# Four of ten top-32 masks move from VectorE to ScalarE in a one-core attention kernel

## The chip, the cores and the metric

The kernel runs as one program on one NeuronCore of a Trainium2 chip. The metric is the device time of one execution in microseconds (us). A core has TensorE (PE, matrix products; PEld is its weight loads), VectorE (DVE), ScalarE (ACT), GpSimd (POOL) and a queue for transfers on SyncE (SP). They run side by side and are ordered by semaphores that the program writes out.

## The reference, cut to what matters

A deformable convolution, two transformer layers and a mixture of experts run on 8 images of 64 channels and 56 x 56 positions. The change touches only the attention of the two layers. Each layer has 64 (image, head) pairs, "heads" below, with 3136 queries, 3136 keys and 8 values per key:

```python
scores = jnp.einsum('bhqd,bhkd->bhqk', q, kk) * scale      # 3136 x 3136 for each head
vals, idx = jax.lax.top_k(scores, k)                       # k = 32
w = jax.nn.softmax(vals, axis=-1)
vg = jnp.take_along_axis(v[:, :, None, :, :], idx[..., None], axis=3)
out = jnp.einsum('bhqk,bhqkd->bhqd', w, vg)
```

The kernel never makes indices. It finds each query's 32nd largest score, marks every key below it in a mask, and lets TensorE add a very large negative number to the marked scores before the exponential.

## The kernel before, in words

`heads` calls `attend` 8 times a layer, each for 8 heads. A head has 25 tiles of 128 queries (the last has 64), so one `attend` has 200 tiles and the program 3200. All of the order is written out by hand in one loop for each engine.

**First half: the threshold.** TensorE (`scores`, L242) multiplies a tile's queries with all keys in four pieces (two banks of 448 keys, two, two, one), always into the same two PSUM banks. ScalarE (`keep`, L371) copies each piece to the ring `S` in SBUF, which has 8 slots of one tile. TensorE may not overwrite the banks before that copy is done, and ScalarE's next copy waits for TensorE. VectorE takes the top 8 of each of 28 chunks of 112 keys (`part_top`, L446), merges these candidates to the 32 largest (`candidates`, L463 to L476), tests for doubt (L480) and writes the mask `Z` (L486), which is 1 where the score is below the 32nd. The merge, the test and the mask of a tile are woven into the next tile's chunk maxima.

**Doubt and search.** The candidates are exact unless a chunk hides a ninth large score or the lower tiers of the chunks hold more than eight. `doubt` (L480) marks rows in which that may be so. TensorE counts the marks of a group of four tiles (`flag`, L250; the last group has five), and three tiles later VectorE reads the count (`check`, L496, L497). If there is a mark, VectorE searches the marked tile anew over all 3136 keys (`search`, L515 to L522). When a check is done, VectorE's queue is drained (L506), and `s_free` gives the group's ring slots back to ScalarE.

**Second half: the output.** It works on 512 queries at a time, a set of four tiles, and runs about eight tiles behind the first half. TensorE computes the transposed scores of 256 keys (`fill`: L280, and L289 for the masks, whose blocks are the stationary operand of 128 x 128 matmuls), ScalarE takes the exponential (`exps`, L392 and L395), and TensorE multiplies with the values after every second unit of this kind (`values`, L325). Two such units are in flight in PSUM: `fill(e+2)` waits for `exps(e)`. There are 80 units for the 100 pieces of a head, so four pieces out of five have a unit behind them. Rarer steps are `shifts`/`shift_rows` (L260, L377), `sums` (L403) and `fold`/`folded` (L335, L410).

**The loop that the change cuts into.** In step `a` ScalarE's queue holds `keep(a)` and then `exps(e)`. TensorE's queue holds `scores(a+1)`, `fill(e+2)` and, for every second unit, `values(e)`. Each engine executes its own queue in order.

Of the kernel before, what the change touches and what calls it, by code (L numbers as in the profile page):

```python
# [62 lines left out]
RANKED = TOP_AT + 8 * CHUNKS  # L63
RING = 8
MASKS = 10
BLOCK = 8
PIECES = (2, 2, 2, 1)
AP = len(PIECES)
# [3 lines left out]
PENDING = 4  # L72
CHECKS = [range(4 * g, 4 * g + 4) for g in range(5)] + [range(20, NT)]
LATE = 3
TERMS, ZERO_TO, MAX_AT = 48, 96, 96


# [26 lines left out]
def attend(nc, m, base, n):  # L104

    bank = m.bank
    names = ("q_in", "v9_in", "v1_in", "a_mm", "a_ev", "s_free", "tops", "step", "found", "viol", "flag_mm", "flag_in",
             "z_done", "part", "maxp", "max_mm", "max_in", "e_mm", "e_exp", "pv", "o_ev", "fold_mm", "os_done", "o_out")
    with semaphores(nc, *names) as sems, nc.Block() as block:
        (q_in, v9_in, v1_in, a_mm, a_ev, s_free, tops, step, found, viol, flag_mm, flag_in,  # L110
         z_done, part, maxp, max_mm, max_in, e_mm, e_exp, pv, o_ev, fold_mm, os_done, o_out) = sems
        psO, psX = bank[6], bank[7]
        flags = psX[32:33, :]
        maxima = psX[MAX_AT:MAX_AT + 3, :]
# [24 lines left out]
        def side(i):  # L139
            return i % 2  # L140
# [1 line left out]
        def slot(t):  # L142
            return t % RING

        def place(i, t):
            return (NT * i + t) % MASKS

        def checks_to(i, t):

# [76 lines left out]
        def _(pe):  # L226
# [37 lines left out]
            def fill(e):  # L264

                s, p = units[e]
                i, g = sets[s]
                w = set_width(g)
                per = QW // w
                if p == 0 and i >= 0:  # L270
                    pe.wait_ge(max_in, max_sets(i) + g + 1)
                    pe.wait_ge(s_free, checks_to(i, set_tiles(g)[-1]))
                    pe.wait_ge(z_done, NT * i + set_tiles(g)[-1] + 1)
                if e >= 2:
                    pe.wait_ge(e_exp, e - 1)

                def shifted(x, k):
                    rows = tile_rows(k)
                    at = w * (x % per)
                    pe.matmul(bank[2 + 2 * (e % 2) + x // per][0:rows, at:at + w],  # L280
                              m.K[0:MAX_AT + 3, side(i), 128 * k:128 * k + rows],
                              m.Q[0:MAX_AT + 3, side(i), QW * g:QW * g + w], start=True, stop=False)

                def masked(x, k):
                    rows = tile_rows(k)
                    for j, t in enumerate(set_tiles(g)):
                        cols = tile_rows(t)
                        at = w * (x % per) + 128 * j
                        mm = pe.matmul(bank[2 + 2 * (e % 2) + x // per][0:rows, at:at + cols],  # L289
                                       m.Z[:, place(i, t), 128 * k:128 * k + rows], m.NEG[:, 0:cols],  # L290
                                       start=False, stop=(j == len(set_tiles(g)) - 1))
# [12 lines left out]
                mm.then_inc(e_mm, 1)  # L304
# [57 lines left out]
        def _(act):  # L362
            def keep(a):
                tile, c = divmod(a, AP)
                i, t = divmod(tile, NT)
                rows, at, w = tile_rows(t), CW * sum(PIECES[:c]), PIECES[c]
                act.wait_ge(a_mm, a + 1)
                if c == 0 and tile >= RING:
                    act.wait_ge(s_free, checks_to(*divmod(tile - RING, NT)))
                    act.wait_ge(z_done, tile - RING + 1)  # L370
                act.copy(m.S[0:rows, slot(tile), at:at + CW * w].rearrange("p (a n) -> p a n", a=w),  # L371
                         m.AB[0:rows, 0:w, 0:CW]).then_inc(a_ev, 1)

            def shift_rows(i, g):
                k = max_sets(i) + g
# [36 lines left out]
            for a in range(SLOTS):  # L412
                if a < NA:
                    keep(a)
                for e in units_at(a):
                    exps(e)
                    if e + 3 in first_unit and e + 3 < NE and sets[units[e + 3][0]][0] >= 0:
                        shift_rows(*sets[units[e + 3][0]])
                    if e - 1 in first_unit[1:]:
                        sums(first_unit.index(e - 1) - 1)  # L420
                    if e - 5 in first_unit[1:]:
                        folded(first_unit.index(e - 5) - 1)
            sums(len(sets) - 1)
            for s in range(len(sets)):
                if first_unit[s + 1] + 5 >= NE:
# [6 lines left out]
        def _(dve):  # L432
# [6 lines left out]
                count[0] += 1  # L439
                op().then_inc(step, 1)  # L440

            def part_top(tile, k):
                rows = tile_rows(tile % NT)
                if k % 8 == 0:
                    dve.wait_ge(a_ev, AP * tile + k // 8 + 1)
                ins = dve.max(m.C[0:rows, tile % 2, TOP_AT + k:RANKED:CHUNKS],  # L446
                              m.S[0:rows, slot(tile), CHUNK * k:CHUNK * k + CHUNK])
                if k == CHUNKS - 1:
                    ins.then_inc(tops, 1)

            def candidates(tile):

# [24 lines left out]

                def doubt():
                    dve.wait_ge(found, tile + 1)
                    dve.scalar_tensor_tensor(m.VI[0:rows, t:t + 1], m.C8[0:rows, t:t + 1], C[:, 7:8],  # L480
                                             m.M8[0:rows, side(i), t, 31:32], ALU.max, ALU.is_ge).then_inc(viol, 1)

                def mask():
                    if mask_freed(tile):
                        dve.wait_ge(e_mm, mask_freed(tile))
                    dve.tensor_scalar(m.Z[0:rows, place(i, t), :], m.S[0:rows, slot(tile), :],  # L486
                                      m.M8[0:rows, side(i), t, 31:32], None, ALU.is_lt, saturate=False).then_inc(z_done, 1)
                return steps + [final, doubt, mask]

            def check(i, g):  # L490

# [6 lines left out]
                dve.wait_ge(flag_in, 2 * done)  # L498
                flagged = nc.vector.value_load(m.FI[32:33, 31:32], min_val=0, max_val=128)
                with nc.vector.If(flagged > 0):  # L500
                    dve.wait_ge(z_done, NT * i + checked[-1] + 1)
                    for t in checked:
                        n_t = nc.vector.value_load(m.FI[32:33, t:t + 1], min_val=0, max_val=128)
                        with nc.vector.If(n_t > 0):
                            search(i, t)
                dve.drain().then_inc(s_free, 1)  # L506

            def search(i, t):
                rows = tile_rows(t)
# [4 lines left out]
                for r in range(1, 4):  # L514
# [1 line left out]
                    dve.drain()  # L516
                    dve.max(M8[:, 8 * r:8 * r + 8], S)  # L517
                    dve.drain()
                Z = m.Z[0:rows, place(i, t), :]
                dve.tensor_scalar(Z, S, M8[:, 31:32], None, ALU.is_lt, saturate=False)  # L520
                dve.drain()
                dve.scalar_tensor_tensor(Z, S, LOW, Z, ALU.is_gt, ALU.mult, saturate=False)  # L522
# [2 lines left out]
            for tile in range(TILES):  # L525
                steps = candidates(tile - 1) if tile else []
                for k in range(CHUNKS):
                    part_top(tile, k)
                    for g in range(len(CHECKS)):
                        before = tile - LATE - CHECKS[g][-1]  # L530
                        if k == 6 and before >= 0 and before % NT == 0:
                            check(before // NT, g)
                    if k % 2 == 1 and steps:
                        steps.pop(0)()
                for remaining in steps:
                    remaining()
            if n:
                for remaining in candidates(TILES - 1):
                    remaining()
                check(n - 1, len(CHECKS) - 1)  # L540


Q_TERMS = ((0, 0, 1, 3), (24, 1, 1, 2), (40, 2, 1, 1))
# [11 lines left out]
def attend_memory(nc, ctx, m):  # L555
    for name, shape, dt in (
            ("Q", [128, 2, TOK], BF16), ("K", [128, 2, TOK], BF16), ("V9", [128, NT * (HD + 1)], F32),
            ("V1", [128, 2, NT, 32], F32), ("S", [128, RING, TOK], F32), ("Z", [128, MASKS, TOK], FP8),
            ("W", [128, 4, 2, QW], F32), ("O4", [128, QW], F32), ("OS", [HD + 1, 2, QW], F32),
            ("C", [128, 2, RANKED], F32), ("C8", [128, NT], F32), ("M8", [128, 2, NT, 32], F32),  # L560
            ("VI", [128, NT], F32), ("FI", [33, 32], I32), ("P", [128, 2, 3, 4], BF16), ("R", [128, 2, 4], F32),
# [4 lines left out]
def heads(nc, m):  # L566

    with ExitStack() as ctx:
        attend_memory(nc, ctx, m)
        with semaphores(nc, "zeroed", "spare", "loaded", "v9_first") as (zeroed, spare, loaded, v9_first), nc.Block() as block:  # L570
            @block.gpsimd
            def _(pool):
                for t in (m.V1, m.Q, m.K, m.Z, m.M8, m.VI):
                    pool.memset(t[:], 0.0).then_inc(zeroed, 1)
                pool.wait_ge(v9_first, 16)
                pool.tensor_copy(m.V1[:, 0, :, 0:HD + 1], m.V9[:, :].rearrange("p (t d) -> p t d", d=HD + 1))
# [14 lines left out]

            @block.vector
            def _(dve):
                dve.wait_ge(zeroed, 6)
                dve.memset(m.K[MAX_AT:MAX_AT + 3, :, :], 1.0)
                dve.tensor_copy(m.identb[:, :], m.ident[:, :])
                dve.tensor_scalar(m.NEG[:, :], m.ident[:, :], -2.0 ** 60, None, ALU.mult)
# [1244 lines left out]
```

## Time and profile before

| | us |
|---|---|
| median of 3 runs | 40355.22 (40340.66 to 40358.04) |
| profiled execution, its own time | 40352.54 |
| its span | 40350.9 |
| DVE busy | 34096.2 (84%) |
| PE busy | 27849.8 (69%) |
| ACT busy | 21427.6 (53%) |
| POOL busy | 2703.4 (7%) |

A busy share is a mean over stages with different limits. Attention fills two stretches of the span, one in each layer; the rest is the convolution, projections, norms, feed-forward and experts. In a row of a timeline the number in square brackets is how long the engine had been idle and which instruction ended that. In a table of windows, PEclk is TensorE's granted clock: 1.00 is 2.4 GHz and 0.50 is 1.2 GHz.

### The profile page before, as it was taken

How to read it: one execution, taken by the hardware profiler on the slowest of the kernel's cores; microseconds unless marked ns; L12 is line 12 of the kernel's file. 1: busy time of each engine (PE TensorE's matmuls, PEld its weight loads, DVE VectorE, ACT ScalarE, POOL GpSimd, SP SyncE). 2: the span in 40 equal slices, each digit the busy share in tenths (PEclk: the TensorE clock that was granted, in tenths of full speed). 3: DMA queues.
4: the chain of work that ended last, by engine and by line, in shares of the span. 5: the costliest groups of instructions: out<-in, count | busy, mean ns of one | idle time of the engine just before them, and what ended most of it. 6: DMA issues, size and time to landing. Idle time of an engine off the chain costs nothing. (4 is left out here: it accounts for less than half of the span.)

```text
span 40350.9 us, 609164 instructions
## 1 busy us (share of the span) xinstructions
PE 27849.8 (69%) x190808; PEld 12177.8 (30%) x190809; DVE 34096.2 (84%) x146975; ACT 21427.6 (53%) x28193; POOL 2703.4 (7%) x5550
## 2 busy tenths in 40 slices
PE   4557776666767767867347677777775777674399
PEld 4533332222323323323123233333332333222122
DVE  5659999999999999999669999999999999996611
ACT  1126665555656656756146566666665666563111
POOL 0000000000000000000000000000000000000000
PEclk7779898888989889989579899999898999887555
DMA  0010000000000000000110000000000000001100
GB/s 36 8 51 5 5 5 4 4 4 4 5 4 5 5 4 5 5 5 5 53 48 5 4 5 5 5 6 5 5 5 4 5 5 5 4 5 42 54 10 6
DMA packets 133064, 453.78 MB, mean 11 GB/s; under 512 B 29244, under 2 KB 85444, under 8 KB 111240
## 3 DMA queue, kind: packets, MB, share of 16 engines
q1 hardware_dynamic: 129256, 410.72, 3.0%
q8 instruction: 1448, 23.72, 0.3%
q14 instruction: 2360, 19.33, 0.2%
HBM read 244.71 MB, written 165.93 MB: 10 GB/s over the span
## 5 line engine op out<-in xcount | busy, mean ns | idle before, releaser
L446 DVE MAX8 C<-S 128x8 f32<-128x112 f32 x89600 | 19150.7, 268 | 1227.6 <-issue 910.5
L371 ACT COPY S<-banks 128x896 f32<-128x896 f32 (+1 forms) x12800 | 10427.7, 815 | 11433.1 <-PE banks L242 7858.2
L242 PE MATMUL banks<-K,Q 96*128 96x448 bf16 x22400 | 6729.3, 371 | 6459.9 <-ACT S L371 5925.8
L392 ACT ACTIVATE W<-banks 128x1024 f32<-128x1024 f32 (+1 forms) x9524 | 9822.5, 1032 | 71.8 <-PE banks L289 71.8
L280 PE MATMUL banks<-Q,K 99*128 99x512 bf16 (+2 forms) x22550 | 6552.9, 376 | 2112.8 <-ACT W L392 2032.7
L325 PE MATMUL banks<-W,V 128*32 128x512 f32 (+1 forms) x45100 | 7085.9, 596 | 142.7 <-ACT W L395 103.6
L289 PE MATMUL banks<-NEG,Z 128*128 128x128 bf16 (+3 forms) x80450 | 6666.5, 227 | 0.0
L289 PEld LDWEIGHTS banks<-NEG,Z 128*128 128x128 fp8e4 (+1 forms) x80450 | 5799.8, 103 | 2576.4 <-issue 474.6
L486 DVE TENSOR_SCALAR Z<-S,M 128x3136 fp8e4<-128x3136 f32 (+1 forms) x3200 | 5871.8, 1835 | 69.9 <-PE banks L289 69.9
L242 PEld LDWEIGHTS banks<-K,Q 96*128 96x128 bf16 x22400 | 1470.8, 99 | 12891.8 <-ACT S L371 8570.4
L280 PEld LDWEIGHTS banks<-Q,K 99*128 99x128 bf16 (+1 forms) x22550 | 1730.1, 101 | 5384.7 <-ACT W L392 3750.0
L471 DVE MAX8 M<-C 128x8 f32<-128x92 f32 x9600 | 2285.9, 238 | 1.7
L472 DVE MATCH_REPLACE8 C<-M,C 128x92 f32<-128x92 f32 x9600 | 2286.3, 238 | 0.0
L204 POOL TENSOR_SCALAR R<-M 128x4 f32<-128x4 f32 (+1 forms) x896 | 205.0, 229 | 29492.9 <-DVE M L476 29492.9
L206 POOL CAST P<-R 128x4 bf16<-128x4 f32 (+1 forms) x1792 | 1771.3, 988 | 116.8
L325 PEld LDWEIGHTS banks<-W,V 128*32 128x32 f32 x45100 | 1268.1, 113 | 1068.8 <-issue 469.7
L1687 DVE TENSOR_TENSOR moe_hw<-moe_hg,banks 128x448 f32<-128x448 f32 x448 | 278.2, 621 | 1514.4 <-ACT moe_hg L1620 1514.4
L818 PE MATMUL banks<-dc_tap,c_group 128*128 128x224 f32 x2800 | 776.9, 362 | 789.4 <-DVE dc_tap L873 789.4
L517 DVE MAX8 M<-S 128x8 f32<-128x3136 f32 (+1 forms) x360 | 1234.0, 3428 | 27.8 <-issue 0.9
L515 DVE MATCH_REPLACE8 S<-M,S 128x3136 f32<-128x3136 f32 (+1 forms) x360 | 1228.3, 3412 | 2.9 <-issue 1.6
L1620 ACT ACTIVATE moe_hg<-banks,moe_b 128x448 f32<-128x448 f32 x448 | 284.0, 634 | 1564.1 <-PE banks L1582 1564.1
L838 ACT ACTIVATE dc_d<-banks,c_omb 128x224 f32<-128x224 f32 x378 | 149.5, 447 | 1801.4 <-PE banks L807 1801.1
(198 smaller groups left out, 19568.6 us busy)
## 6 DMA issues: line engine op xcount, KB each, us to landing
q<-ln_o SPq DMA_DIRECT2D x20, 1568.0 KB, 5.1
ln_x<-y SPq DMA_DIRECT2D x16, 1568.0 KB, 6.1
K<-k_parts SPq DMA_DIRECT2D x130, 147.0 KB
Q<-q_parts SPq DMA_DIRECT2D x130, 147.0 KB
q_parts<-pj_parts SPq DMA_DIRECT2D x24, 784.0 KB, 4.7
k_parts<-pj_parts SPq DMA_DIRECT2D x24, 784.0 KB, 7.8
V<-v_rows SPq DMA_DIRECT2D x130, 112.5 KB, 7.4
v_rows<-pj_vt SPq DMA_DIRECT2D x8, 1800.0 KB, 11.8
```

The costliest lines, as they stand in the source:

```text
L206: chained(lambda a=a: pool.tensor_copy(P[:, a, :], R[:, a, :]))
L242: mm = pe.matmul(bank[j][0:rows, 0:CW], m.Q[0:ZERO_TO, side(i), 128 * t:128 * t + rows], m.K[0:ZERO_TO, side(i), at:at + CW], start=True, ...
L280: pe.matmul(bank[2 + 2 * (e % 2) + x // per][0:rows, at:at + w], m.K[0:MAX_AT + 3, side(i), 128 * k:128 * k + rows], m.Q[0:MAX_AT + 3, sid ...
L289: mm = pe.matmul(bank[2 + 2 * (e % 2) + x // per][0:rows, at:at + cols], m.Z[:, place(i, t), 128 * k:128 * k + rows], m.NEG[:, 0:cols], st ...
L325: mm = pe.matmul(psO[32 * (k % 4):32 * (k % 4) + 32, 0:w], m.V1[0:rows, side(i), k, :], m.W[0:rows, at, x // per, w * (x % per):w * (x % p ...
L371: act.copy(m.S[0:rows, slot(tile), at:at + CW * w].rearrange("p (a n) -> p a n", a=w), m.AB[0:rows, 0:w, 0:CW]).then_inc(a_ev, 1)
L392: ins = act.activation(m.W[:, e % 4, 0:n_banks, :], m.AB[:, b:b + n_banks, :], ACT.Exp)
L446: ins = dve.max(m.C[0:rows, tile % 2, TOP_AT + k:RANKED:CHUNKS], m.S[0:rows, slot(tile), CHUNK * k:CHUNK * k + CHUNK])
L471: steps.append(lambda r=r: chained(lambda: dve.max(top(r), few)))
L472: steps.append(lambda r=r: chained(lambda: dve.match_replace(few, top(r), few, LOW)))
L486: dve.tensor_scalar(m.Z[0:rows, place(i, t), :], m.S[0:rows, slot(tile), :], m.M8[0:rows, side(i), t, 31:32], None, ALU.is_lt, saturate=Fa ...
L517: dve.max(M8[:, 8 * r:8 * r + 8], S)
```

## The change

- `MAKERS = "DADADDADAD"` gives each tile, by its number modulo 10, an engine that makes its mask: VectorE (D, six of ten) or ScalarE (A, four of ten).
- ScalarE's masks are `Relu(threshold - score)`, a positive number instead of 1, in bfloat16 slots of their own (`ZA`). VectorE's masks stay 0 or 1 in fp8 (`Z`). There are still ten slots.
- ScalarE makes the mask of tile T-4 right after its last copy of tile T, and ahead of the exponential of that step. It waits for `found`, the threshold of tile T-4.
- The counter `z_done` becomes `z_dve` and `z_act` (and `z_pool`, not used). TensorE ahead of a set, ScalarE ahead of a ring slot, and VectorE ahead of a search wait for both.
- The doubt test is strict: greater than the 32nd, no longer greater or equal.
- The drain after a check goes. `s_free` is now incremented by the chunk maximum that follows the check; the check stands at the same place in VectorE's queue.

```diff
+MAKERS = "DADADDADAD"
+BEHIND = 4
+        def mask_at(tile):
+            x = tile % MASKS
+            k = sum((MAKERS[y] == "A") == (MAKERS[x] == "A") for y in range(x))
+            return (m.ZA if MAKERS[x] == "A" else m.Z)[:, k, :]
+
+        def masks_made(engine, tile):
+            for sem, kind in ((z_dve, "D"), (z_act, "A"), (z_pool, "P")):
+                made = sum(maker(x) == kind for x in range(tile + 1))
+                if made:
+                    engine.wait_ge(sem, made)
...
+            def mask(tile):
+                i, t = divmod(tile, NT)
+                rows = tile_rows(t)
+                act.wait_ge(found, tile + 1)
+                if mask_freed(tile):
+                    act.wait_ge(e_mm, mask_freed(tile))
+                act.activation(mask_at(tile)[0:rows, :], m.S[0:rows, slot(tile), :], ACT.Relu,
+                               bias=m.M8[0:rows, side(i), t, 31:32], scale=-1.0).then_inc(z_act, 1)
...
             for a in range(SLOTS):
                 if a < NA:
                     keep(a)
+                    if a % AP == AP - 1 and a >= AP * BEHIND and maker(a // AP - BEHIND) == "A":
+                        mask(a // AP - BEHIND)
                 for e in units_at(a):
                     exps(e)
...
-                    dve.scalar_tensor_tensor(m.VI[0:rows, t:t + 1], m.C8[0:rows, t:t + 1], C[:, 7:8],
-                                             m.M8[0:rows, side(i), t, 31:32], ALU.max, ALU.is_ge).then_inc(viol, 1)
+                    dve.tensor_scalar(m.VI[0:rows, t:t + 1], m.C8[0:rows, t:t + 1], C[:, 7:8],
+                                      m.M8[0:rows, side(i), t, 31:32], ALU.max, ALU.is_gt).then_inc(viol, 1)
...
-                return steps + [final, doubt, mask]
+                return steps + [final, doubt] + ([mask] if maker(tile) == "D" else [])
...
                 with nc.vector.If(flagged > 0):
-                    dve.wait_ge(z_done, NT * i + checked[-1] + 1)
+                    masks_made(dve, NT * i + checked[-1])
...
-                dve.drain().then_inc(s_free, 1)
```

ScalarE's queue inside one `attend`, before, with what each instruction waits for. L371 is the copy of a piece to the ring (the 128x448 one is the last of its tile), L392 the exponential:

```order
L371 COPY S<-banks 128x896 [waits a_mm]
L392 ACTIVATE W<-banks 128x1024 [waits pv,e_mm]
L410 COPY OS<-banks 9x512 [waits fold_mm]
L371 COPY S<-banks 128x448 [waits a_mm]
L392 ACTIVATE W<-banks 128x1024 [waits pv,e_mm]
L371 COPY S<-banks 128x896 [waits a_mm] x2
```

The same place in the changed kernel, where L384 is that copy, L414 the exponential and L393 the new mask:

```order
L384 COPY S<-banks 128x896 [waits a_mm]
L414 ACTIVATE W<-banks 128x1024 [waits pv,e_mm]
L432 COPY OS<-banks 9x512 [waits fold_mm]
L384 COPY S<-banks 128x448 [waits a_mm]
L393 ACTIVATE ZA<-S,M8 128x3136 [waits e_mm,found]
L414 ACTIVATE W<-banks 128x1024 [waits pv,e_mm]
L384 COPY S<-banks 128x896 [waits a_mm] x2
```

One instruction over 3136 columns stands between the last copy of the tile and the exponential; nothing else has moved.

VectorE's queue at a check, before. L496 and L497 read the count, L503 is the first instruction of the conditional part, L515 the first of a search:

```order
L496 CAST FI<-banks 1x4 [waits flag_mm]
L497 TENSOR_REDUCE FI<-banks 1x1
L499 TENSOR_LOAD FI [waits flag_in]
L500 COMPARE_AND_BRANCH
L503 TENSOR_LOAD FI [waits z_done]
L504 COMPARE_AND_BRANCH
L515 MATCH_REPLACE S<-M,S 128x3136
```

The same place in the changed kernel (L525 and L526 read the count, L532 begins the conditional part, L543 a search):

```order
L525 CAST FI<-banks 1x4 [waits flag_mm]
L526 TENSOR_REDUCE FI<-banks 1x1
L528 TENSOR_LOAD FI [waits flag_in]
L529 COMPARE_AND_BRANCH
L532 TENSOR_LOAD FI [waits z_act,z_dve]
L533 COMPARE_AND_BRANCH
L543 MATCH_REPLACE S<-M,S 128x3136
```

The order is the same. What is new is that a flagged check waits for ScalarE's masks too.

## Rows read from the trace of the kernel before

**Rows 1.** Windows over the attention of each layer: length, busy us (instructions), PEclk.

```profile
2881.00:19165.00 16284.00, 11766.83 (x88211) 4976.94 (x88210) 15240.84 (x68661) 10116.03 (x12947) 1270.20 (x2752) 0.89 0.02 5
20676.00:36785.00 16109.00, 11770.11 (x88064) 4988.56 (x88062) 15084.15 (x68595) 10106.49 (x12936) 1270.13 (x2752) 0.90 0.02 5
```

**Rows 2.** The same windows for L520 alone, one for each search.

```profile
2881.00:19165.00 16284.00, 116.74 (x63) 0.89 0.02 5
20676.00:36785.00 16109.00, 105.59 (x57) 0.90 0.02 5
```

**Rows 3.** A window without searches: PE, PEld, DVE, ACT, POOL; then L486 alone.

```profile
5240.00:6290.00 1050.00, 849.10 (x6464) 359.67 (x6463) 1005.81 (x5031) 745.60 (x955) 94.98 (x206) 0.96 0.02 5
...
5240.00:6290.00 1050.00, 217.34 (x119) 0.96 0.02 5
```

**Rows 4.** Waits in that window: us in total, times, longest.

```profile
ACT S L371 <- PE banks L242: 289.0, 259, 3.1
...
PE banks L280 <- ACT W L392: 80.8, 192, 0.7
DVE C L446 <- issue: 31.1, 23, 1.7
ACT S L371 <- issue: 8.5, 4, 2.1
```

**Rows 5.** Timeline of ScalarE: start, us.

```profile
16400.70 1.03 ACT L392 ACTIVATE W<-banks 128x1024 f32<-128x1024 f32 x1
16401.62 0.91 ACT L371 COPY S<-banks 128x896 f32<-128x896 f32 x1
...
16404.25 0.53 ACT L371 COPY S<-banks 128x448 f32<-128x448 f32 x1 [1.24 <-PE banks L242]
16404.68 1.03 ACT L392 ACTIVATE W<-banks 128x1024 f32<-128x1024 f32 x1
16406.59 0.91 ACT L371 COPY S<-banks 128x896 f32<-128x896 f32 x1 [0.88 <-PE banks L242]
```

**Rows 6.** Timeline of TensorE in the same stretch.

```profile
16401.88 0.59 PE L280 MATMUL banks<-Q,K 99*128 99x512 bf16 x2 [0.47 <-ACT W L392]
...
16402.85 1.07 PE L325 MATMUL banks<-W,V 128*32 128x512 f32 x8
16403.85 0.36 PE L242 MATMUL banks<-K,Q 96*128 96x448 bf16 x1
...
16406.39 0.60 PE L280 MATMUL banks<-Q,K 99*128 99x512 bf16 x2
```

**Rows 7.** Groups of ScalarE's instructions by shape: busy us, mean ns.

```profile
L1197 ACT ACTIVATE ln_s<-banks,c_eps 128x448 f32<-128x448 f32 x168 | 104.3, 621 | 42.3 <-PE banks L1157 42.1
L1201 ACT ACTIVATE ln_q<-ln_c 128x448 f32<-128x448 f32 x168 | 96.6, 576 | 1123.7 <-DVE ln_c L1188 1123.7
...
L844 ACT ACTIVATE dc_hy<-dc_d 128x2016 f32<-128x2016 f32 x14 | 26.1, 1867 | 0.0
```

**Rows 8.** Windows of TensorE alone around a fall of its clock: busy us, PEclk.

```profile
11973.10:11976.50 3.40, 1.91 (x15) 1.00 0.00 0
11976.50:11979.90 3.40, 3.40 (x20) 0.53 0.00 0
```

**Rows 9.** Timeline of both engines in the second of these windows.

```profile
11976.55 0.94 ACT L371 COPY S<-banks 128x896 f32<-128x896 f32 x1
...
11977.68 1.94 PE L325 MATMUL banks<-W,V 128*32 128x512 f32 x8
...
11980.14 0.53 ACT L371 COPY S<-banks 128x448 f32<-128x448 f32 x1 [1.71 <-PE banks L242]
```

**Rows 10.** Timeline of ScalarE at the end of a search.

```profile
12024.40 0.90 ACT L371 COPY S<-banks 64x896 f32<-64x896 f32 x1 [26.05 <-issue]
```

**Rows 11.** Groups of TensorE's weight loads, whole span.

```profile
L289 PEld LDWEIGHTS banks<-NEG,Z 128*128 128x128 fp8e4 (+1 forms) x80450 | 5799.8, 103 | 2576.4 <-issue 474.6
...
L280 PEld LDWEIGHTS banks<-Q,K 99*128 99x128 bf16 (+1 forms) x22550 | 1730.1, 101 | 5384.7 <-ACT W L392 3750.0 <-issue 983.8 <-ACT W L395 97.6
```

More of the change, by code:

```diff
@@ L107, in attend @@
     names = ("q_in", "v9_in", "v1_in", "a_mm", "a_ev", "s_free", "tops", "step", "found", "viol", "flag_mm", "flag_in",
-             "z_done", "part", "maxp", "max_mm", "max_in", "e_mm", "e_exp", "pv", "o_ev", "fold_mm", "os_done", "o_out")
+             "z_dve", "z_act", "z_pool", "part", "maxp", "max_mm", "max_in", "e_mm", "e_exp", "pv", "o_ev", "fold_mm", "os_done", "o_out")
     with semaphores(nc, *names) as sems, nc.Block() as block:
         (q_in, v9_in, v1_in, a_mm, a_ev, s_free, tops, step, found, viol, flag_mm, flag_in,
-         z_done, part, maxp, max_mm, max_in, e_mm, e_exp, pv, o_ev, fold_mm, os_done, o_out) = sems
+         z_dve, z_act, z_pool, part, maxp, max_mm, max_in, e_mm, e_exp, pv, o_ev, fold_mm, os_done, o_out) = sems
         psO, psX = bank[6], bank[7]
@@ L143, in slot, with maker @@
             return t % RING
-        def place(i, t):
-            return (NT * i + t) % MASKS
+        def maker(tile):
+            return MAKERS[tile % MASKS]
+        def mask_at(tile):
[7 more added lines that the diff above has]
+                    engine.wait_ge(sem, made)
         def checks_to(i, t):
@@ L272, in fill @@
                     pe.wait_ge(s_free, checks_to(i, set_tiles(g)[-1]))
[L273 removed]
+                    masks_made(pe, NT * i + set_tiles(g)[-1])
                 if e >= 2:
@@ L289, in masked @@
                         mm = pe.matmul(bank[2 + 2 * (e % 2) + x // per][0:rows, at:at + cols],
-                                       m.Z[:, place(i, t), 128 * k:128 * k + rows], m.NEG[:, 0:cols],
+                                       mask_at(NT * i + t)[:, 128 * k:128 * k + rows], m.NEG[:, 0:cols],
                                        start=False, stop=(j == len(set_tiles(g)) - 1))
@@ L369, in keep @@
                     act.wait_ge(s_free, checks_to(*divmod(tile - RING, NT)))
-                    act.wait_ge(z_done, tile - RING + 1)
+                    masks_made(act, tile - RING)
                 act.copy(m.S[0:rows, slot(tile), at:at + CW * w].rearrange("p (a n) -> p a n", a=w),
                          m.AB[0:rows, 0:w, 0:CW]).then_inc(a_ev, 1)
+            def mask(tile):
[6 more added lines that the diff above has]
+                               bias=m.M8[0:rows, side(i), t, 31:32], scale=-1.0).then_inc(z_act, 1)
             def shift_rows(i, g):
@@ L422, in _ @@
                         folded(first_unit.index(e - 5) - 1)
+            for tile in range(max(TILES - BEHIND, 0), TILES):
+                if maker(tile) == "A":
+                    mask(tile)
             sums(len(sets) - 1)
@@ L440, in chained, with part_top @@
                 op().then_inc(step, 1)
-            def part_top(tile, k):
+            def part_top(tile, k, checked=False):
                 rows = tile_rows(tile % NT)
@@ L449, in part_top @@
                     ins.then_inc(tops, 1)
+                if checked:
+                    ins.then_inc(s_free, 1)
             def candidates(tile):
@@ L485, in mask @@
                         dve.wait_ge(e_mm, mask_freed(tile))
-                    dve.tensor_scalar(m.Z[0:rows, place(i, t), :], m.S[0:rows, slot(tile), :],
-                                      m.M8[0:rows, side(i), t, 31:32], None, ALU.is_lt, saturate=False).then_inc(z_done, 1)
-                return steps + [final, doubt, mask]
+                    dve.tensor_scalar(mask_at(tile)[0:rows, :], m.S[0:rows, slot(tile), :],
+                                      m.M8[0:rows, side(i), t, 31:32], None, ALU.is_lt, saturate=False).then_inc(z_dve, 1)
+                return steps + [final, doubt] + ([mask] if maker(tile) == "D" else [])
             def check(i, g):
@@ L518, in search @@
                     dve.drain()
-                Z = m.Z[0:rows, place(i, t), :]
+                Z = mask_at(NT * i + t)[0:rows, :]
                 dve.tensor_scalar(Z, S, M8[:, 31:32], None, ALU.is_lt, saturate=False)
@@ L527, in _ @@
                 for k in range(CHUNKS):
-                    part_top(tile, k)
+                    checked = False
                     for g in range(len(CHECKS)):
                         before = tile - LATE - CHECKS[g][-1]
-                        if k == 6 and before >= 0 and before % NT == 0:
+                        if k == 7 and before >= 0 and before % NT == 0:
                             check(before // NT, g)
+                            checked = True
+                    part_top(tile, k, checked)
                     if k % 2 == 1 and steps:
@@ L540, in _ @@
                 check(n - 1, len(CHECKS) - 1)
+                dve.drain().then_inc(s_free, 1)
 Q_TERMS = ((0, 0, 1, 3), (24, 1, 1, 2), (40, 2, 1, 1))
@@ L557, in attend_memory @@
             ("Q", [128, 2, TOK], BF16), ("K", [128, 2, TOK], BF16), ("V9", [128, NT * (HD + 1)], F32),
-            ("V1", [128, 2, NT, 32], F32), ("S", [128, RING, TOK], F32), ("Z", [128, MASKS, TOK], FP8),
+            ("V1", [128, 2, NT, 32], F32), ("S", [128, RING, TOK], F32), ("Z", [128, MASKS - MAKERS.count("A"), TOK], FP8), ("ZA", [128, MAKERS.count("A"), TOK], BF16),
             ("W", [128, 4, 2, QW], F32), ("O4", [128, QW], F32), ("OS", [HD + 1, 2, QW], F32),
@@ L572, in _ @@
             def _(pool):
-                for t in (m.V1, m.Q, m.K, m.Z, m.M8, m.VI):
+                for t in (m.V1, m.Q, m.K, m.Z, m.ZA, m.M8, m.VI):
                     pool.memset(t[:], 0.0).then_inc(zeroed, 1)
@@ L593, in _ @@
             def _(dve):
-                dve.wait_ge(zeroed, 6)
+                dve.wait_ge(zeroed, 7)
                 dve.memset(m.K[MAX_AT:MAX_AT + 3, :, :], 1.0)
```

## The prediction, made before the changed kernel ran

> **What bounds the kernel now.** I read the windows first. Attention takes 16284 + 16109 = 32393 us of the span, and DVE is busy 94% of it [rows 1]. That makes VectorE look like the only bound, and the change takes work from it. A share does not say how much room the next engine has, so I then looked for a stretch without a search, where the pace is steady: 1050 us with 119 masks begun, the outer ones cut, so I count 118.5 tiles and 8.86 us a tile [rows 3]. DVE is busy 1005.8 us there and idle 31 us behind its checks [rows 4]; the 13 us left are smaller gaps. VectorE never waits for data, so it sets 8.86.
>
> The reader should then look at who else would have had time. ScalarE is busy 745.6 us and waits 289 us for TensorE's scores, but only 8.5 us (four times) for anything else; those four are the waits for a free ring slot, the only place where VectorE holds it up [rows 3, 4]. TensorE has no wait for VectorE in the list, but it waits for ScalarE, 80.8 us ahead of L280 alone [rows 4]. So ScalarE and TensorE hold each other in a loop that by itself needs 8.86 - 8.5/118.5 = 8.79 us a tile. Two limits stand 0.07 us apart. Work taken from VectorE can win at most that; work given to the loop is paid wherever it is not hidden inside it.
>
> Searches come on top. With x us a search and y us for the start and end of each `attend`, layer one gives 16284 - 1600 x 8.86 = 2108 = 63x + 8y and layer two 1933 = 57x + 8y [rows 1, 2]: x = 29, y = 34. Sum: 3200 x 8.86 + 120 x 29 + 16 x 34 = 32376, within 0.1% of 32393.
>
> **The change part by part.** *Masks off VectorE.* 1280 of 3200 masks, 1.83 us each [rows 3], are 2340 us of DVE time, 0.73 us a tile. VectorE's need falls to about 8.1 us a tile. Since the loop stands at 8.79, this is worth 0.07 us a tile, 224 us in all. The rest turns into waiting.
>
> *Masks on ScalarE.* No row shows a Relu over 3136 columns. From 448 to 2016 columns an activation grows from 576 to 1867 ns, 0.823 ns a column; 1120 more columns give 2.79 us, and a bias read per partition adds 621 - 576 = 45 ns [rows 7]: 2.84 us. Neighbours on ScalarE overlap by 0.11 us (0.91 us copies are followed after 0.8 us), so each mask holds the queue for 2.75 us. The bounds are close: 2.6 (no bias price, more overlap) to 2.95. The Trainium skill, "ScalarE: Activation LUTs", section "What ACT_TABLE_LOAD costs", gives 280 + 0.833 N ns for this form, 2.89 us; that would add 0.05 us. Its "Rules for kernel authors" also say to do a relu on VectorE. No row compares the two on one shape; whether that advice holds depends on the loop, as follows.
>
> How much is hidden? One pass of the loop at full clock: the exponential starts at 16400.70, its end releases L280 at 16401.88, then L325 at 16402.85, the next scores at 16403.85, and the copy at 16404.25 after 1.24 us of waiting [rows 5, 6]. A mask ahead of that exponential moves the whole chain by 2.75 us; the later wait stays, because TensorE stops as well. In the next step TensorE is the later one: L280 starts at 16406.39 without having waited, and the copy waits 0.88 us. With a mask between 16404.25 and 16404.68 the exponential starts at 16407.43 and the next copy at 16408.35 instead of 16406.59, so 1.76 us are paid and 1.0 is hidden. A step of the first kind has `values` behind its own `fill`. Counting units against sets (13 units each, pairs end at odd numbers and at the last), five of the ten masks of a head fall into each kind. Mean: (2.75 + 1.76)/2 = 2.25 us a mask.
>
> *TensorE's clock.* During a mask TensorE has only one scores step to do; from its end to the end of mask and exponential it stands idle for some 3.2 us. In the trace a stretch at 2.4 GHz in which TensorE idled 1.5 us was followed by one at 0.53, nearly all of it at 1.2 GHz [rows 8]. In it L325 took 1.94 us instead of 1.07, and from copy to copy passed 3.59 us, where the full clock shows 2.63 from 16401.62 to 16404.25 with a unit and its values in between [rows 5, 6, 9]. So a fall costs about 1.0 us, or 1.3 if the steps compared are not quite alike. I expect it behind three masks of four: 0.8 us a mask. Bounds: 0 (the idle falls where it is not seen) and 2.6 (the clock stays down twice as long). The Trainium skill, "TensorE: Matmul & The Clock Gate", Part 1, says the throttled state is the default and activity lifts it; the windows agree, and by it alone I could not size this term.
>
> A mask thus costs 3.05 us, 1.22 us a tile: the loop goes from 8.79 to 10.01.
>
> *Strict test.* A search is now made only where a hidden candidate is above the 32nd. Counting on the reference's own scores, the inclusive test marks 63 and 57 tiles in the two layers, the counts in the trace [rows 2]; the strict one marks 53 and 46. 99 searches are left, in 90 flagged checks.
>
> *What a search costs then.* While VectorE searches, ScalarE runs up to the first ring slot of the checked group and stops; the trace shows such a stop of 26.05 us [rows 10]. With the loop as the limit the stop is what counts. New is that VectorE must first wait for ScalarE's masks of the group. If the group's last A tile is its last tile (4 of 10), that mask stands at the very end of what ScalarE may do, and ScalarE then stops for the full 29 us; if it is one tile earlier (4 of 10), for about 22; two tiles earlier (2 of 10), for 14. Mean 23. 90 x 23 + 9 x 26 (second searches in one check) = 2300 us.
>
> *Edits that I cost at nothing.* The drain gone and the new form of the doubt test save or cost tenths of a microsecond on VectorE, which then has 1.9 us a tile to spare. Mask blocks in bfloat16: TensorE loads fp8 blocks in 103 ns and bfloat16 ones in 101 [rows 11]. ScalarE's wait for `found` of tile T-4: it is due only when VectorE is over three tiles behind, which a starving VectorE is not. TensorE's wait for the masks of a set: ScalarE has made them at least a step earlier.
>
> **Sum.** 3200 x 10.01 + 2300 + 16 x 34 = 34876 us of attention, 2483 more than 32393. On the profiled execution's 40352.5 us this is 42836; that execution lies 3 us under the median of the runs, so I predict 42840 us, 6.2% slower.
>
> **The rivals.** A: *forecast.* The loop pays 2.2 to 4.1 us a mask: without any fall of the clock 9.7 us a tile and 41800; with 2.75 us on every mask and 1.3 for the clock 10.43 and 44200. Chance 62%. For it: the 8.5 us against 289 in [rows 4]. Against it: the two steps that I timed are two of a hundred.
>
> B: *faster.* TensorE has work left over whenever ScalarE turns to a mask and does it meanwhile, so that the 289 us that ScalarE now waits are used up and the loop pays under 1.1 us a mask. That is the turning point: 3200 x (8.79 + 0.4 d) + 2844 = 32393 gives d = 1.1. For it: ScalarE is idle 2.4 us a tile for TensorE, twice what the masks need (1.1 a tile). Against: TensorE itself waits for ScalarE's exponentials. At d = 0.6 the time is 39700; at 0 it is 38930, the floor. 14%.
>
> C: *half hidden.* The waits absorb about half a mask and the clock stays: d = 1.6, 3200 x 9.43 + 2844 = 33020, so 40980. 16%.
>
> D: *the clock collapses.* Every mask sends TensorE to 1.2 GHz for twice as long: d = 2.75 + 2.6, 10.93 us a tile, 45790. For it: up to 3.2 us idle after each mask. Against: at 1.2 GHz TensorE is busy all of the stretch [rows 8], and the clock of the whole window stays at 0.96 [rows 3], so falls are short. 6%.
>
> The remaining 2% lie within 0.2% of the time before, about what runs of this kernel can tell from no change. Faster is B, 14%; slower is A, C and D, 84%. From 40300 to 44200 leaves out B, D and little else.
>
> **What would show it.** Right: a stretch without searches runs at 9.7 to 10.4 us a tile; VectorE's largest new wait is L473 for ScalarE's copy, some 1.5 to 2 us a tile; ScalarE's wait for ring slots is gone but at searches; L393 takes 2.8 to 2.9 us; PEclk in such a stretch falls from 0.96 to about 0.9; 99 instructions of L548. Wrong: a pace under 9.2 us a tile, or ScalarE's waits for scores shrinking by as much as its masks add, or PEclk under 0.8.

## The result, and the profile after

The changed kernel takes 42922.71 us (median of 4 runs, 42920.91 to 42925.86), the one before 40349.79 us beside it: a ratio of 1.0638 (95% interval 1.0619 to 1.0656), 6.4% slower. 42840 was predicted, 83 us less, with a range of 40300 to 44200.

First the windows over the two layers' attention in the changed kernel (columns as in [rows 1]), then the same windows for L548, one for each search:

```profile
2883.00:20465.00 17582.00, 12490.75 (x88080) 5197.72 (x88079) 14010.72 (x67911) 11862.08 (x13577) 950.90 (x2752) 0.85 0.01 4
21990.00:39356.00 17366.00, 12449.55 (x88064) 5188.51 (x88064) 13827.26 (x67834) 11861.25 (x13576) 950.86 (x2752) 0.86 0.01 4
...
2883.00:20465.00 17582.00, 98.20 (x53) 0.85 0.01 4
21990.00:39356.00 17366.00, 85.21 (x46) 0.86 0.01 4
```

Attention is 34948 us against 32393 [rows 1], 2555 more; that is nearly all of the difference of 2573. VectorE has 2487 us less to do there (14010.72 + 13827.26 against 15240.84 + 15084.15), and the stretch is longer all the same. The searches are 53 and 46, as counted.

A stretch without searches, all engines, then the ring copies alone, and the waits in it (L384 is the copy, L255 the scores, L293 the head of `fill`, L414 the exponential, L525 reads a check's count, L473 is a chunk maximum):

```profile
10110.00:11690.00 1580.00, 1214.63 (x8755) 509.15 (x8753) 1254.99 (x6699) 1173.31 (x1348) 93.78 (x271) 0.90 0.02 5
...
10110.00:11690.00 1580.00, 516.47 (x635) 0.90 0.02 5
```

```profile
ACT S L384 <- PE banks L255: 396.5, 330, 4.3
...
PE banks L293 <- ACT W L414: 212.1, 271, 3.0
DVE FI L525 <- PE banks L263: 191.6, 38, 6.9
...
DVE C L473 <- ACT S L384: 73.1, 67, 2.6
```

635 copies are 158.75 tiles: 9.95 us a tile, where it was 8.86 [rows 3]. VectorE was busy 1005.8 of 1050 us and now is 1255 of 1580. ScalarE waits 2.50 us a tile for scores, 2.44 before [rows 4]: on balance its waiting time has absorbed nothing. (That is a balance only: what a mask hides and what the slower clock adds to the waits cannot be told apart in it.) TensorE's wait for the exponential ahead of `fill`, 0.68 us a tile before, is now 1.34. The granted clock of the stretch has gone from 0.96 to 0.90. Between two levels that is 8% and 20% of the time at 1.2 GHz, 0.7 and 2.0 us a tile, or about 3.2 us more for each mask.

VectorE's and ScalarE's other instructions have not slowed beside the masks: over the whole span a chunk maximum takes 268 ns in both kernels, a ring copy of 896 columns 909 and 908 ns, an exponential 1037 and 1034 ns.

One mask from near, ScalarE and TensorE in the changed kernel (L393 is the mask, L338 `values`), and TensorE's windows around it:

```profile
10504.78 0.52 ACT L384 COPY S<-banks 128x448 f32<-128x448 f32 x1
10505.21 2.90 ACT L393 ACTIVATE ZA<-S,M 128x3136 bf16<-128x3136 f32 x1
10508.02 1.00 ACT L414 ACTIVATE W<-banks 128x1024 f32<-128x1024 f32 x1
```

```profile
10509.07 0.61 PE L293 MATMUL banks<-Q,K 99*128 99x512 bf16 x2 [2.03 <-ACT W L414]
...
10512.59 1.80 PE L338 MATMUL banks<-W,V 128*32 128x512 f32 x8
```

```profile
10507.00:10510.40 3.40, 1.37 (x13) 1.00 0.01 2
10510.40:10513.80 3.40, 3.13 (x19) 0.55 0.00 0
```

The mask holds ScalarE's queue for 2.81 us (2.75 predicted). TensorE idles 2.03 us while the clock is still at 2.4 GHz, and the second of the two windows, which begins 1.33 us after that, runs almost wholly at 1.2 GHz (0.55). In it `values` (L338) takes 1.80 us instead of 1.07 [rows 6].

### The profile page after: what moved, and what is told of

It reads as the page before. It is cut to its first block and busy times, and to the rows that moved or that the text cites. A ratio compares the mean times of both kernels' runs of the same rounds, so it can differ in the third digit from the quotient of the medians.

```text
span 42919.4 us, 612128 instructions
## 1 busy us (share of the span) xinstructions
PE 29264.6 (68%) x190808; PEld 12606.0 (29%) x190809; DVE 31608.8 (74%) x145464; ACT 24936.7 (58%) x29473; POOL 2064.9 (5%) x5552
## 5 line engine op out<-in xcount | busy, mean ns | idle before, releaser
L473 DVE MAX8 C<-S 128x8 f32<-128x112 f32 x89600 | 19091.5, 267 | 2487.0 <-ACT S L384 1594.4
L384 ACT COPY S<-banks 128x896 f32<-128x896 f32 (+1 forms) x12800 | 10413.1, 814 | 10764.2 <-PE banks L255 8176.6
L255 PE MATMUL banks<-K,Q 96*128 96x448 bf16 x22400 | 6970.4, 383 | 5570.4 <-ACT S L384 5120.6
L293 PE MATMUL banks<-Q,K 99*128 99x512 bf16 (+2 forms) x22550 | 6947.5, 395 | 4243.2 <-ACT W L414 4166.9
L414 ACT ACTIVATE W<-banks 128x1024 f32<-128x1024 f32 (+1 forms) x9524 | 9788.8, 1028 | 72.0 <-PE banks L302 72.0
L338 PE MATMUL banks<-W,V 128*32 128x512 f32 (+1 forms) x45100 | 7570.6, 634 | 137.8 <-ACT W L417 102.1
L302 PE MATMUL banks<-NEG,Z 128*128 128x128 bf16 (+3 forms) x48250 | 6489.4, 234 | 0.0
L302 PE MATMUL banks<-NEG,ZA 128*128 128x128 bf16 (+1 forms) x32200 | 5616.1, 234 | 0.0
L302 PEld LDWEIGHTS banks<-NEG,Z 128*128 128x128 fp8e4 (+1 forms) x48250 | 4664.7, 108 | 1652.3 <-issue 545.0
L255 PEld LDWEIGHTS banks<-K,Q 96*128 96x128 bf16 x22400 | 1517.1, 100 | 12294.7 <-ACT S L384 7529.2
L293 PEld LDWEIGHTS banks<-Q,K 99*128 99x128 bf16 (+1 forms) x22550 | 1749.2, 104 | 7815.7 <-ACT W L414 6231.8
L393 ACT ACTIVATE ZA<-S,M 128x3136 bf16<-128x3136 f32 x1280 | 3734.4, 2918 | 52.3 <-DVE M L505 52.3
L515 DVE TENSOR_SCALAR Z<-S,M 128x3136 fp8e4<-128x3136 f32 (+1 forms) x1920 | 3526.6, 1837 | 314.0 <-PE banks L302 313.9
L302 PEld LDWEIGHTS banks<-NEG,ZA 128*128 128x128 bf16 (+1 forms) x32200 | 3361.2, 106 | 1174.4 <-issue 376.2
L525 DVE CAST FI<-banks 1x4 int32<-1x4 f32 (+1 forms) x768 | 118.9, 155 | 3664.7 <-PE banks L263 3664.3
L338 PEld LDWEIGHTS banks<-W,V 128*32 128x32 f32 x45100 | 1327.1, 117 | 1187.1 <-issue 665.3
```

Of the source, the lines that this page charges most:

```text
L255: mm = pe.matmul(bank[j][0:rows, 0:CW], m.Q[0:ZERO_TO, side(i), 128 * t:128 * t + rows], m.K[0:ZERO_TO, side(i), at:at + CW], start=True, ...
L338: mm = pe.matmul(psO[32 * (k % 4):32 * (k % 4) + 32, 0:w], m.V1[0:rows, side(i), k, :], m.W[0:rows, at, x // per, w * (x % per):w * (x % p ...
L393: act.activation(mask_at(tile)[0:rows, :], m.S[0:rows, slot(tile), :], ACT.Relu, bias=m.M8[0:rows, side(i), t, 31:32], scale=-1.0).then_in ...
L414: ins = act.activation(m.W[:, e % 4, 0:n_banks, :], m.AB[:, b:b + n_banks, :], ACT.Exp)
L515: dve.tensor_scalar(mask_at(tile)[0:rows, :], m.S[0:rows, slot(tile), :], m.M8[0:rows, side(i), t, 31:32], None, ALU.is_lt, saturate=False ...
```

## The experiments

All times are medians of a kernel's runs; the kernel before was run beside each group (40323.79 to 40331.23 us). The changed kernel's 42922.71 us comes from the first group, where the kernel before took 40349.79; these 26 us (0.07%) are in every difference taken from it. A price "a mask" is a difference divided by 1280 masks.

**The strict test alone.** The kernel before with one word changed:

```diff
-                                             m.M8[0:rows, side(i), t, 31:32], ALU.max, ALU.is_ge).then_inc(viol, 1)
+                                             m.M8[0:rows, side(i), t, 31:32], ALU.max, ALU.is_gt).then_inc(viol, 1)
```

> The kernel before with the strict doubt test alone. My theory (a search costs what VectorE is held up, 29 us, and 99 instead of 120 are left): 40350 - 21 x 29 = 39740 us. Rival (searches are mostly absorbed by the ring, or the count does not fall): 40350, no change.

39711.75 us, ratio 0.9847 (0.9831 to 0.9864). 21 searches fewer won 619 us, 29.5 us each.

**All masks on VectorE, the rest of the change kept.**

```diff
-MAKERS = "DADADDADAD"
+MAKERS = "DDDDDDDDDD"
```

> The changed kernel with all ten masks on VectorE again, so the strict test and the release of ring slots by the next maximum are what is left of the change. My theory: as e1_strict less the drains, 768 of about 0.1 us, so 39670 to 39740 us; the whole loss of the changed kernel is then the placement of the masks. Rival (the new counters and the release by the next maximum cost something): over 40000.

39721.54 us, ratio 0.9848 (0.9832 to 0.9865). The drain and the release by the next maximum are worth nothing that can be measured. All of the loss lies in who makes the masks: 42922.71 - 39721.54 = 3201 us, which the strict test's 619 us then reduced.

**ScalarE's instruction cut to 8 columns**, its place and waits kept; most marks of four tiles in ten are left out.

```diff
-                act.activation(mask_at(tile)[0:rows, :], m.S[0:rows, slot(tile), :], ACT.Relu,
+                act.activation(mask_at(tile)[0:rows, 0:8], m.S[0:rows, slot(tile), 0:8], ACT.Relu,
```

> The changed kernel, but ScalarE's mask instruction covers 8 of 3136 columns; it stands in the same place with the same waits. Most of the marks of four tiles in ten are left out, so the second layer works on other numbers and may have a few searches more or less. My theory (the length of the instruction is what is paid; VectorE relieved of 1280 masks gains only 0.07 us a tile): the loop at about 8.85 us a tile, 39400 us, from 39100 to 39700. Rival 1 (what is paid is the hand-over: waits of TensorE and VectorE for ScalarE's masks): it stays above 42000. Rival 2 (VectorE was the real bound and its 0.73 us a tile come through once ScalarE is free): near 37500.

39755.99 us, ratio 0.9859 (0.9843 to 0.9876), with 106 searches. Brought to 99 at 29 us it is 39553. (As measured, 39756 lies 56 us above the range expected; brought to 99 searches it lies inside.) Against the kernel with all masks on VectorE this is about 170 us less, though VectorE is rid of 1280 masks, 2340 us of its work. The prediction had 224 for that relief. Relief and hand-over are seen only together here: the hand-over with its waits costs less than the relief wins.

**Half the columns**, 0:1568 in the same line.

> The changed kernel, with ScalarE's mask instruction over 1568 of 3136 columns, the rest of these marks left out (as in e3_no_scalar_masks). About 1.5 us of ScalarE's queue instead of 2.8. My theory: 1.5 us paid in half of the steps and about 0.5 in the others, and 0.3 for the clock, so 1.3 us a mask and 40850 us, from 40500 to 41300. Rival (ScalarE's waits absorb short instructions in full): as e3_no_scalar_masks, 39400. Rival (a fixed price for each mask, such as a fall of the clock): above 41800.

40877.41 us, ratio 1.0134 (1.0117 to 1.0151), 107 searches, so 40645 at 99. From nothing to half a mask costs 0.85 us a mask, from half to all (42923 - 40645)/1280 = 1.78 us. The traces show where the first part is paid. I timed each stretch from ScalarE's copy ahead of one mask to its copy ahead of the next (75 in an `attend`, median over the 16) in the kernel with 8 columns and in this one. Where TensorE has `values` in the step of the mask, which is the prediction's first kind and half of the places, a stretch is 1.61 us longer, in the others 0.42 us. The expectation said 1.5 and 0.5. (Timed so, the mean is 1.0, a little above the 0.85 from the whole times.) The second 1568 columns take ScalarE 1.31 us (L393 takes 2.92 us, with half the columns 1.61) and cost 1.78, more than their length; the clock falls further with them (granted over the whole run 0.845 with 8 columns, 0.836 with half, 0.813 with all). All of it together: (42923 - 39553)/1280 = 2.63 us a mask.

**The mask behind the exponential of its step.**

```diff
                 if a < NA:
                     keep(a)
-                    if a % AP == AP - 1 and a >= AP * BEHIND and maker(a // AP - BEHIND) == "A":
-                        mask(a // AP - BEHIND)
                 for e in units_at(a):
                     exps(e)
+                if a < NA and a % AP == AP - 1 and a >= AP * BEHIND and maker(a // AP - BEHIND) == "A":
+                    mask(a // AP - BEHIND)
+                for e in units_at(a):
                     if e + 3 in first_unit and e + 3 < NE and sets[units[e + 3][0]][0] >= 0:
                         shift_rows(*sets[units[e + 3][0]])
```

The rarer copies of the step (`shift_rows`, `sums`, `folded`) now come behind the mask.

> The changed kernel, with ScalarE's mask behind the exponential of its step instead of ahead of it. My theory: TensorE's fill and values then run during the mask, the next copy is late by 1.7 us in both kinds of steps instead of 2.75 and 1.76, and the clock falls less often: about 2.1 us a mask, 41870 us, from 41500 to 42300. Rival (what counts is only how long ScalarE's queue is held): 42920, no change.

41781.16 us, ratio 1.0363 (1.0345 to 1.0380). The same instructions one place later cost 1142 us less: 1.74 us a mask instead of 2.63. What counts is what stands behind the mask, not only how long it holds the queue. Timed as above against the changed kernel, the stretches whose mask step has `values` became 1.74 us shorter and the others did not change (0.03 us longer): the gain lies where TensorE needs the exponential for `values` before it can go on to the next scores.

**Work for TensorE during the mask**, which nobody reads.

```diff
                     scores(a + 1)
+                    if a % AP == AP - 1 and a >= AP * BEHIND and maker(a // AP - BEHIND) == "A":
+                        for _ in range(24):
+                            pe.matmul(psX[64:96, 0:128], m.identb[:, 0:32], m.NEG[:, :], start=True, stop=True)
```

> The changed kernel with 24 matmuls of 128 columns that nobody reads in TensorE's queue behind the scores of each step that has a ScalarE mask, so that TensorE works through most of its idle time there. My theory (falls of the clock behind the idle time cost 0.66 to 0.8 us a mask): 42000 us, from 41800 to 42400, with the granted clock of attention up to about 0.95. Rival (the clock is no part of it): 42920, or a little more where the 24 matmuls are in the way.

41755.81 us, ratio 1.0355 (1.0338 to 1.0372), 44 us quicker than the range expected. TensorE executes 29952 matmuls more, and the kernel is 1167 us quicker, 0.91 us a mask. One such stretch, then a window over most of the first layer's attention in this kernel, and the same window in the changed one; the granted clock is 0.91 against 0.85:

```profile
16297.96 1.51 PE L359 MATMUL banks<-NEG,identb 128*32 128x128 bf16 x24
```

```profile
2880.00:18900.00 16020.00, 11846.95 (x96565) 5431.76 (x96564) 13161.70 (x63641) 11098.97 (x12720) 887.90 (x2568) 0.91 0.02 4
```

```profile
2880.00:18900.00 16020.00, 11364.08 (x80132) 4728.65 (x80132) 12769.18 (x61794) 10789.38 (x12349) 863.05 (x2500) 0.85 0.01 4
```

The falls of the clock behind the masks are thus a price of their own. The 0.91 us a mask may contain some falls that the kernel had without such masks; the last experiment shows that there are some.

**No searches at all**, before and after (rows in doubt keep their candidates).

```diff
-                with nc.vector.If(flagged > 0):
+                with nc.vector.If(flagged > 127):
```

> The kernel before, with a search never started (its condition is never true), so rows in doubt keep their candidates. My theory: 120 searches at 29 us are 3480, so 36870 us. If VectorE's own work were all there is (25.8 us a search), 37250. Rival (ScalarE's and TensorE's time during a search is made up later): well above 38000.

36788.08 us, ratio 0.9123 (0.9105 to 0.9142): (40323.79 - 36788.08)/120 = 29.5 us a search.

> The changed kernel, with a search never started. The prediction's 23 us for each flagged check gives 42920 - 2300 = 40620 us; the windows of the changed kernel's two layers give 26 us a search and 40350. Rival (a search costs more than before, since VectorE waits for ScalarE's masks first; 35 us or more): below 39500.

40047.66 us, ratio 0.9932 (0.9912 to 0.9952): (42922.71 - 40047.66)/99 = 29.0 us a search. That is more than both figures expected. I had 23 for most of them. Here is one flagged check in the changed kernel: VectorE (L525 reads the count, L543 begins the search), then ScalarE and TensorE in the same place:

```profile
3027.60 0.15 DVE L525 CAST FI<-banks 1x4 int32<-1x4 f32 x1 [4.60 <-PE banks L263]
...
3040.48 0.09 DVE L543 MATCH_VALUE_LOAD S<-M,S 128x8 f32 x1 [12.65 <-issue]
```

```profile
3034.67 2.93 ACT L393 ACTIVATE ZA<-S,M 128x3136 bf16<-128x3136 f32 x1
...
3068.34 0.91 ACT L384 COPY S<-banks 128x896 f32<-128x896 f32 x1 [29.22 <-issue]
```

```profile
3069.30 0.93 PE L255 MATMUL banks<-K,Q 96*128 96x448 bf16 x2 [30.10 <-ACT S L384]
```

VectorE is idle 12.65 us. ScalarE's mask ends at 3037.60, 2.9 us before the search begins; the loads and branches of the conditional part lie in that rest. Meanwhile ScalarE runs into the end of the ring and stops for 29.22 us. This is one of the longest such waits (13.5 us is the longest). Over the whole program VectorE's idle time ahead of searches is 458.2 us, with all masks on VectorE 259.5, so waiting for ScalarE's masks adds some 2 us a search on average.

Behind the stop TensorE starts at 1.2 GHz (a scores pair takes 0.93 us, not 0.55), which the prediction had left out. ScalarE's stops over the whole program are 2419.9 us and 125.2 more behind the chunk maximum that gives slots back, some 26 for a search (the kernel without searches has no such stops), where the prediction had 2300 us. ScalarE's waits for scores are 8176.6 us with searches and 7999.8 without, 1.8 us a search, which is what the slow restart can account for. The last 1.5 us of the 29 lie in smaller waits.

**One mask of ten on ScalarE**, behind the exponential: `MAKERS = "DDDADDDDDD"` in the kernel with the mask behind.

> As e5_mask_behind, but only one mask in ten is ScalarE's. Against e1_strict, e5 paid (41781 - 39712 + 224)/1280 = 1.8 us a mask. My theory (the loop had 0.07 us a tile to spare, and every mask beyond that is paid): loop 8.79 + 0.18 = 8.97 us a tile, 0.11 over VectorE's 8.86, so 39712 + 350 = 40060 us. Rival (a few masks fit into ScalarE's waiting time and VectorE's relief of 0.18 us a tile comes through): 39400 or less.

40052.5 us, ratio 0.9933 (0.9916 to 0.9950), 341 us more than the strict test alone. As the kernel stands, even the first mask finds no room.

**The same, with idle time filled.**

```diff
                         values(e)
+                if a < NA and a % AP == AP - 1 and a >= AP * BEHIND and maker(a // AP - BEHIND) == "A":
+                    for _ in range(12):
+                        pe.matmul(psX[64:96, 0:128], m.identb[:, 0:32], m.NEG[:, :], start=True, stop=True)
+                elif a < NA and not units_at(a):
+                    for _ in range(8):
+                        pe.matmul(psX[64:96, 0:128], m.identb[:, 0:32], m.NEG[:, :], start=True, stop=True)
```

> As e9_one_mask, with matmuls that nobody reads in TensorE's idle time: 12 in the steps with a ScalarE mask and 8 in the steps that have no unit, one step in five. My theory (falls of the clock also slow the loop of the kernel before, about one in five tiles at some 1 us): the loop falls to about 8.8 us a tile and the time to 39400 or 39500, under e1_strict. Rival (VectorE or the matmuls themselves stand in the way): 39700 or more.

39398.31 us, ratio 0.9768 (0.9751 to 0.9784): the quickest version, 0.8% under the strict test alone and 2.3% under the kernel before.

**Four masks behind the exponential, with 16 such matmuls** in place of the 12 and none elsewhere.

> As e5_mask_behind (four masks in ten), with 16 matmuls that nobody reads behind TensorE's work of each step that has a ScalarE mask. If the clock still falls behind these masks, and costs what e6_filler won back (0.9 us a mask), 40600 us; if the mask behind the exponential had already done away with most of these falls, 41500 to 41800. I expect 41100, between the two.

41299.85 us, ratio 1.0241 (1.0224 to 1.0258). The filler wins 481 us here and 1167 with the mask ahead of the exponential. The later place has taken away part of the falls: the granted clock of the whole run is 0.813 in the changed kernel, 0.828 with the mask behind, 0.847 with the filler added to that, and 0.857 with mask ahead and filler. But this filler is also shorter and stands elsewhere, and the runs do not tell the two apart. The time is 200 us above the 41100 expected.

**The 8 matmuls alone**, with all masks on VectorE.

> As e2_all_vector (all masks on VectorE, strict test), with the 8 matmuls that nobody reads in TensorE's queue in the steps without a unit, as in e10_one_mask_filler. My theory (VectorE sets the pace of 8.86 us a tile here, so a quicker loop gains nothing): 39720 as e2_all_vector, from 39600 to 39800. Rival (what e10 won came from the matmuls alone): 39400.

39479.08 us, ratio 0.9790 (0.9773 to 0.9806): 242 us under the kernel with all masks on VectorE, where I had expected none. This expectation failed. In the waits of the kernel before stands one that I had counted under "smaller gaps":

```profile
DVE FI L496 <- PE banks L250: 356.7, 246, 4.8
```

It is the wait of the line that reads a check's count. In the kernel with all masks on VectorE, and then with the filler added, the same wait is

```profile
DVE FI L525 <- PE banks L263: 339.0, 246, 5.0
```

```profile
DVE FI L528 <- PE banks L263: 111.2, 124, 1.5
```

228 us went from it, nearly as much as the time fell. So VectorE did not set the pace of 8.86 us quite alone: in one check of three (246 of 768) it waited for the loop. Falls of the clock go with it: in the kernel with all masks on VectorE the clock had been down at some time in the 20 us ahead of 71% of these waits, and ahead of 36% of the checks without one. Of the 323 us between the quickest version and the one with all masks on VectorE, ScalarE's mask is worth at most 81.

## Why the prediction was right

**The bound.** Right in the main: the loop of TensorE and ScalarE had next to nothing to spare. VectorE's relief won 170 us (224 said), and with a tenth of the masks on ScalarE the kernel was already 341 us slower. Wrong in a detail: "VectorE never waits for data". It did, for flags, some 357 us in all, and 201 us for copies (L446 for L371, 110 times). So the loop was in part the bound already, beside VectorE.

**The price of a mask.** 3.05 us was the sum of 2.25 for the queue and 0.8 for the clock. Measured are 2.63 in all, 0.42 too high: this is the step that was mis-sized. Filling TensorE's idle time gives back 0.91, which leaves 1.72 for the queue. The clock's part was sized nearly right, the queue's too high. The two kinds of steps are real. Stretch by stretch, from the kernels without searches, a mask costs 3.12 us in a step with `values` (2.75 + 0.8 = 3.55 said) and 2.27 in the others (1.76 + 0.8 = 2.56 said), 2.69 in the mean. Each is 0.3 to 0.4 below what the one pass gave that I had timed for its kind; how queue and clock share that within a kind stays open. The length of the instruction was sized at 2.84 us and is 2.92 (mean of 1280). Of the two rows whose difference of 45 ns was taken for the bias one reads PSUM and the other SBUF [rows 7], so they were no clean pair.

**The searches.** Their number was right, 99. Their price was not: 2300 us predicted, 2875 measured. The stop was sized at 23 us, where 29.0 are paid, about as much as before the change (29.5): the stops alone are some 26, and the restart was left out.

**The sum.** Between the two kernels without searches lie 3260 us; the prediction had (10.01 - 8.86) x 3200 = 3680 for this, 420 too many. For the searches it had 3480 - 2300 = 1180 us of gain, measured are 3536 - 2875 = 661, so 519 too much. The two errors have opposite signs, and that is why the total is off by 83 us only. That is luck. A total that agrees to 0.2% is no proof of its terms.

**Signs named beforehand.** The pace (9.95, said 9.7 to 10.4), PEclk (0.90), 99 searches, and no wait for a ring slot in a stretch without searches came as said. L393, at 2.92 us, lies just above the 2.8 to 2.9 said. VectorE's largest new wait did not: it is not the copy (1594.4 us, 0.5 a tile, where 1.5 to 2 were said) but the check, in the list of the changed kernel

```profile
DVE FI L525 <- PE banks L263: 3664.3, 737, 8.0
```

since TensorE issues the flags of a group only with the scores of a later tile. The waiting VectorE finds itself there first. While the loop is the limit this costs nothing.

**The rivals.** *Faster* fell: its turning point was 1.1 us a mask, and 2.63 are paid. *Half hidden* gave 1.6 us a mask, with about half absorbed and the clock kept. The clock did fall, so it is wrong as it stands, but with the falls filled 1.72 is left, and about 1 of the 2.75 us is then hidden. *The clock collapses* fell too: PEclk is 0.90, and 2.63 us are far from 5.35.

The page rule that a relu belongs on VectorE (the Trainium skill, "ScalarE: Activation LUTs", "Rules for kernel authors") came out right here, though not for the speed of the instruction alone (2.92 us against 1.84, fp32 read, where the page's reason is bf16): the queue it was put into was the one without room. The price of 2.89 us, an estimate from the same page's "What ACT_TABLE_LOAD costs", is within 1% of the row.

## What to carry to other kernels

Before moving work to an engine that looks half idle, see what its idle time waits for. If it is another engine that in turn waits for it, the two form a loop, the idle time is part of it, and an instruction put in is paid except where the other side is late. If it must be put in, put it behind what the other engine waits for: here one place later saved 2.7%, all of it in the steps where the other engine had more work hanging on that wait. And try the parts of a change one by one: a word in a comparison, hidden under a loss of 8%, was worth 1.5%.

## What the runs showed of the hardware

- Matmuls that nobody reads made a kernel quicker, by 2.7% with ScalarE's masks and by 0.6% without, by keeping the granted clock up (first layer 0.85 to 0.91 in the first case, whole run 0.847 to 0.864 in the second). The Trainium skill, "TensorE: Matmul & The Clock Gate", Part 1, says that activity lifts the throttle; these runs agree.
- An idle time of 2.03 us, in a window where TensorE was busy 1.37 of 3.40 us at 2.4 GHz, was followed by one almost wholly at 1.2 GHz (0.55).
- Mask blocks in bfloat16 load as quickly as in fp8, side by side in one accumulation (106 and 108 ns in the changed kernel's groups):

```profile
L302 PEld LDWEIGHTS banks<-NEG,Z 128*128 128x128 fp8e4 (+1 forms) x48250 | 4664.7, 108 | 1652.3 <-issue 545.0
...
L302 PEld LDWEIGHTS banks<-NEG,ZA 128*128 128x128 bf16 (+1 forms) x32200 | 3361.2, 106 | 1174.4 <-issue 376.2
```
